# A graph kernel's second layer summed in transposed form in four PSUM banks, its first product moved ahead, its norm applied by ScalarE

## What is computed

```python
def layer_0(x, A, W1, b1, W2, b2):
    h = relu(A @ (x @ W1) + b1)
    return relu(A @ (h @ W2) + b2)

def layer_1(x, A, W1, W2, W3):
    A2 = A @ A; A3 = A2 @ A
    return (A @ x @ W1 + A2 @ x @ W2 + A3 @ x @ W3) / 3.0

x = layernorm(x + layer_0(x, adj, ...))     # over the 128 features, eps 1e-5
x = layernorm(x + layer_1(x, adj, ...))
```

## Time and profile before

| | value |
|---|---|
| median of three runs | 263.14 us |
| the profiled execution's own time | 263.5 us |
| its span, first to last instruction | 261.9 us |
| TensorE busy (1144 matmuls) | 245.7 us, 94% |
| VectorE busy | 204.5 us, 78% |
| ScalarE busy | 180.0 us, 69% |
| GpSimd busy | 11.8 us, 5% |
| moved by DMA | 19.43 MB, nearly all in the first 50 us |

### The profile page before, as it was taken

One profiled execution on the slowest core, in us unless ns is written; L12 is line 12 of the kernel. 1 busy time (PEld: TensorE's weight loads), 2 busy tenths in 40 slices (PEclk: granted clock), 3 DMA queues, 4 the chain that ended last, 5 costly groups with the idle time before them and its releaser, 6 DMA issues.

```text
span 261.9 us, 3653 instructions
## 1 busy us (share of the span) xinstructions
PE 245.7 (94%) x1144; PEld 201.4 (77%) x1144; DVE 204.5 (78%) x398; ACT 180.0 (69%) x302; POOL 11.8 (5%) x16
## 2 busy tenths in 40 slices
PE   0998999999999999999999999999999999999990
PEld 0766878787888867788888888888888888888870
DVE  1998888886777999999757595874796777779955
ACT  3889898987667658667766666776676677766520
POOL 1000000000000220220000000000000000022022
PEclk9999999999999999999999999999999999999998
DMA  5999999500000000000000000000000000001111
GB/s 165 372 404 406 403 404 406 219 3 0 0 0 4 1 0 0 0 3 0 1 0 4 0 0 0 3 0 0 1 3 1 0 3 0 0 0 41 43 40 40
DMA packets 10818, 19.43 MB, mean 74 GB/s; under 512 B 1200, under 2 KB 1712, under 8 KB 10800
## 3 DMA queue, kind: packets, MB, share of 16 engines
q1 hardware_dynamic: 10800, 19.21, 19.5%
HBM read 18.15 MB, written 1.05 MB: 73 GB/s over the span
## 4 chain that ended last, share of the span: by engine, by line
PE 79%; DVE 6%; SPq 4%; DMA 3%; issue 3%; POOL 2%; ACT 1%; POOLq 0%; DVEq 0%; ACTq 0%
PE sums L292 24%; PE sums L323 23%; PE sums L324 23%; PE weighted L280 5%; DMA adj<-a_t 3%; SPq L192 3%; DVE ring_low L509 2%; PE turned L277 2%; POOL rstd L225 2%; PE lifted L241 1%; DVE stats L434 1%; DVE nodes L450 1%; SPq L194 1%; SPq L200 1%; ACT ring_high L403 1%
## 5 line engine op out<-in xcount | busy, mean ns | idle before, releaser
L509 DVE TENSOR_TENSOR ring_low<-adj,ring_high 128x512 fp32r<-128x512 f32 x240 | 157.8, 687 | 43.1 <-PE sums L292 28.2
L403 ACT ACTIVATE ring_high<-adj 128x512 fp32r<-128x512 f32 x240 | 147.0, 630 | 36.5 <-PE sums L324 28.1
L323 PE MATMUL sums<-ring_high,operand_high 128*128 128x512 f32 x240 | 96.0, 400 | 7.1 <-DVE operand_low L464 6.9
L292 PE MATMUL sums<-ring_low,operand_high 128*128 128x512 f32 x240 | 94.5, 394 | 1.4 <-DVE ring_low L509 1.3
L324 PE MATMUL sums<-ring_high,operand_low 128*128 128x512 f32 x240 | 94.3, 393 | 0.0
L323 PEld LDWEIGHTS sums<-ring_high,operand_high 128*128 128x128 f32 x240 | 45.5, 190 | 17.1 <-DVE operand_low L464 7.9
L292 PEld LDWEIGHTS sums<-ring_low,operand_high 128*128 128x128 f32 x240 | 45.3, 189 | 12.7 <-DVE ring_low L509 3.0
L324 PEld LDWEIGHTS sums<-ring_high,operand_low 128*128 128x128 f32 x240 | 45.6, 190 | 9.0
L323 PE MATMUL sums<-resident_high,operand_high 128*128 128x512 f32 x80 | 33.2, 416 | 0.0
L292 PE MATMUL sums<-resident_low,operand_high 128*128 128x512 f32 x80 | 31.3, 391 | 0.0
L324 PE MATMUL sums<-resident_high,operand_low 128*128 128x512 f32 x80 | 31.2, 390 | 0.0
(11 more groups left out here) (34 smaller groups left out, 78.1 us busy)
## 6 DMA issues: line engine op xcount, KB each, us to landing
adj<-a_t SPq DMA_DIRECT2D x48, 256.0 KB, 9.1
resident_raw<-a_t SPq DMA_DIRECT2D x16, 256.0 KB, 9.2
nodes<-x_rows SPq DMA_DIRECT2D x4, 256.0 KB, 6.0
out_rows<-nodes SPq DMA_DIRECT2D x3, 256.0 KB, 2.5
out_rows<-nodes SPq DMA_DIRECT2D x2, 128.0 KB, 1.9
par<-params SPq DMA_DIRECT2D x1, 192.0 KB, 9.1
par<-params SPq DMA_DIRECT2D x1, 129.0 KB, 8.1
```

The costliest lines, as they stand in the source:

```text
L292: used = nc.tensor.matmul(sums[:, c, :], operand_high[:, hop % 2, k, :], a_low, start=False, stop=(k == TILES - 1))
L323: nc.tensor.matmul(sums[:, c, :], y_high, a_high, start=(k == 0), stop=False)
L403: nc.scalar.activation(ring_high[:, n % RING, :], adj[:, c, j * STREAMED + i, :], ACT.Copy).then_inc(high_ready, 1)
L509: nc.vector.tensor_tensor(ring_low[:, n % RING, :], adj[:, c, j * STREAMED + i, :], ring_high[:, n % RING, :].bitcast(F32), ALU.subtract). ...
```

## The change

Hop 0: x is loaded transposed together with W1 (`lead_in`), and TensorE forms x W1 first, 16 fp32 products of 128 x 128 in five groups of 1, 3, 4, 4 and 4 tiles (`X_GROUPS`). The group for tiles `first` to `last` is multiplied ahead of tile `first` - 2, and its high and low parts are made ahead of tile `first` - 1, straight from PSUM. The lifts and the separate relu are gone; the evacuation applies bias and relu, and the products by W2 come four tiles after the chunk. The first block of A is issued by ScalarE. `x_rows`, for the residual, is loaded after A. Nine fp32 products on a zeroed buffer (`WARM`) stand ahead of everything on TensorE.

Layer 1: the four banks `filters` collect W1ᵀ(A x)ᵀ + W2ᵀ(A² x)ᵀ in transposed form. For this hops 2 and 3 get one tile more per chunk (`WIDE`, a 17th, streamed): the chunk's sum is split from PSUM into a ring slot and multiplied by the split weight, three products of 128 x 512. The post of hop 2 is four transposes, that of hop 3 four products by W3, whose result is the operand of hop 4; hop 4 sums onto `filters`, its evacuation scales by 1/3, and its post is four transposes. The additions L429 of hops 2 and 3 are gone. Only hop 2 keeps the interleaved order of tiles.

All hops: a tile's three products are now issued together, operand low by A high, high by high, and then at once operand high by A low, with the wait for `low_ready` ahead of it.

Norm: VectorE also forms minus the mean; GpSimd forms a shift, minus the mean times rstd, after the power; ScalarE applies scale and shift to four node tiles (Identity with a scale and a bias read per partition) ahead of item 12. Only the last chunk's halves are still applied by VectorE.

```diff
+X_GROUPS = ((0, 1), (1, 4), (4, 8), (8, 12), (12, 16))
+WARM = 9
+def wide_after(hop, c):
+    return {(2, 0): 9, (2, 1): 11}.get((hop, c), 7)
 def post_step(hop, c):
-    return end_of(hop, c) + (SECOND_AFTER if hop == 0 else POST_AFTER[c])
+    return end_of(hop, c) + (8 if (hop, c) == (2, 1) else 4)
...
+            for n in range(whole_groups):
+                if n:
+                    pool.wait_ge(normalised, n)
+                root(n, slice(0, TPC))
+                pool.wait_ge(rstd_ready, n + 1)
+                nc.gpsimd.tensor_tensor(shift[:], neg_mean[:], rstd[:], ALU.mult).then_inc(shift_ready, 1)
...
+            def first_products(g):
+                pe.wait_ge(lead_sems[g], 16)
+                if g >= 2:
+                    pe.wait_ge(operand_low_ready, g - 1)
+                first, last = X_GROUPS[g]
+                for t in range(first, last):
+                    done = nc.tensor.matmul(x_bank(g)[:, t - first, :], lead[:, 1 + t, :], lead[:, 0, :],
+                                            start=True, stop=True)
+                done.then_inc(first_multiplied, 1)
...
+                nc.tensor.matmul(bank, y_low, a_high, start=first, stop=False)
+                used = nc.tensor.matmul(bank, y_high, a_high, start=False, stop=False)
+                if i < STREAMED:
+                    used.then_inc(high_used, 1)
+                    pe.wait_ge(low_ready, n + 1)
...
+                used = nc.tensor.matmul(bank, y_high, a_low, start=False, stop=last)
...
+            pe.wait_ge(warm_ready, 1)
+            for _ in range(WARM):
+                nc.tensor.matmul(turned[:, 0, :], chunk_t[:, 0:P], chunk_t[:, 0:P], start=True, stop=True)
...
+                        if max(first - 2, 0) == k or (first == 1 and k == 0):
+                            first_products(g)
...
+            def x_tiles(g):
+                first, last = X_GROUPS[g]
+                act.wait_ge(first_multiplied, g + 1)
+                nc.scalar.activation(operand_high[:, 0, first:last, :], x_bank(g)[:, 0:last - first, :], ACT.Copy
...
+            def norm_apply(hop, c):
+                act.wait_ge(shift_ready, residuals(hop, c))
+                for t in range(TPC):
+                    tile = nodes[:, c * TPC + t, :]
+                    last = nc.scalar.activation(tile, tile, ACT.Identity, bias=shift[:, t:t + 1],
+                                                scale=rstd[:, t:t + 1])
+                last.then_inc(normalised, 1)
...
+                for hop, c in posts(n, 5):
+                    if hop in NORMED:
+                        norm_apply(hop, c)
...
+                        if max(first - 1, 0) == k:
+                            x_tiles(g)
```

More of the change, by code:

```diff
@@ L30, with tile_order, all_steps @@
 ACT = mybir.ActivationFunctionType
[L32 to L41, removed]
-    early = TILES - TPC
[L43 to L52, removed]
+W2, B1, B2 = 0, D, D + 1
+V3 = B2 + 1
+PARAMS = V3 + D
+def tile_order(hop):
+    if hop != 2:
+        return [(hop, c, k) for c in range(CHUNKS) for k in range(TILES)]
+    early = TILES - TPC
+    order = [(hop, c, k) for c in (0, 1) for k in range(early)]
+    order += [(hop, c, k) for c in (0, 1) for k in range(early, TILES)]
+    return order + [(hop, c, k) for c in (2, 3) for k in range(TILES)]
+def wide_after(hop, c):
+    return {(2, 0): 9, (2, 1): 11}.get((hop, c), 7)
+def all_steps():
+    order = [step for hop in range(HOPS) for step in tile_order(hop)]
+    after = {order.index((hop, c, TILES - 1)) + wide_after(hop, c): (hop, c, WIDE)
+             for hop in (2, 3) for c in range(CHUNKS)}
+    steps = []
+    for at, step in enumerate(order):
+        steps.append(step)
+        if at in after:
+            steps.append(after[at])
+    return steps
+STEPS = all_steps()
 def streamed(k):
@@ L194, in load, with lead_part @@
                     sp.dma_start(resident_raw[:, c, j, :], a_t[c, :, k, :]).then_inc(resident_in[c][j], 16)
[L196 to L200, removed]
+            def lead_part(g):
+                first, last = X_GROUPS[g]
+                part = slice(first + (g > 0), last + 1)
+                sp.dma_start(lead[:, part, :], lead_in[:, part, :]).then_inc(lead_sems[g], 16)
+            lead_part(0)
+            for k in range(1, TILES):
+                if k == 1:
+                    lead_part(1)
+                elif k % TPC == 2 and k // TPC + 2 < len(X_GROUPS):
+                    lead_part(k // TPC + 2)
+                elif k == TILES - TPC:
+                    sp.dma_start(par[:, W2:V3], params[:, W2:V3]).then_inc(layer_0_in, 16)
                 load(0, k)
-            sp.dma_start(par[:, W1:V1], params[:, W1:V1]).then_inc(layer_0_in, 16)
             for c in range(1, CHUNKS):
@@ L222, in _, with root @@
             pool.wait_ge(exponent_ready, 1)
[L223 to L228, removed]
+            def root(n, part):
+                pool.wait_ge(variance_ready, n + 1)
@@ L232, in _ @@
+            for half in range(HALVES):
+                root(whole_groups + half, slice(half * half_tiles, (half + 1) * half_tiles))
         @block.tensor
         def _(pe):
-            def lift(c):
-                pe.wait_ge(chunk_evacuated, c + 1)
-                if c == 0:
-                    pe.wait_ge(layer_0_in, 16)
[L239 to L242, removed]
@@ L411, in _ @@
+                    nc.scalar.activation(ring_high[:, n % RING, :], source, ACT.Copy).then_inc(high_ready, 1)
+                    n += 1
+                elif hop == 0:
+                    act.wait_ge(resident_in[c][j], 16)
+                    nc.scalar.activation(resident_high[:, c, j, :], resident_raw[:, c, j, :], ACT.Copy
+                                         ).then_inc(resident_high_ready, 1)
+            for n in range(ITEMS, ITEMS + OVERHANG):
+                visits(n)
             act.wait_ge(chunk_summed, HOPS * CHUNKS)
```

434 lines of the change are left out of this document (212 added, 222 removed).

## The result

The changed kernel takes 265.96 us (median, 265.36 to 266.12) against 263.12 (263.04 to 263.2) of the kernel before: ratio 1.0104, 95% interval 1.0086 to 1.0121. It is slower by 1%; 264.7 was forecast. The profiled execution is the fastest of the four, 265.36 us with a span of 263.6. Its span is 1.7 us over that of before, where the sum of the prediction had 1.6.

The account below looks back on a forecast made before the run. TensorE, busy 94% of the span, was taken to bound the kernel. The four parts, 0.1 - 2.15 + 3.75 - 0.1 = +1.6 us on the median of 263.14, gave 264.7 us, range 259.6 to 267.2.

Parts of the forecast that it names:

- Part 1: Start and hop 0: removed lifts and warm-up pay for x W1 and its loop between engines; +0.1 us.
- Rival (b): Chunk 0: the x loop costs nothing as loads hold TensorE there anyway; 2.8 us less, 261.9 us; chance 0.12.
- Part 2: Counted TensorE work after hop 0: fourth lift gone, wide tiles added, posts cheaper; -2.15 us.
- Part 3: Norms of hops 1 and 4: application on ScalarE delays ring items, TensorE waits; 5.6 against 1.85 before, +3.75 us.
- Rival (a): Norm: chain short enough, stalls only 1.0 to 2 us in all; 260.6 us; chance 0.28.
- Rival (d): Norm: Identity needs another activation table, two loads per norm, 14 in all; about 280 us; chance 0.02.
- two things eat this: Hop 1 norm's 0.4 us spare: eaten by item 14's low product standing 0.69 us earlier and by application on ScalarE.
- the power's earlier start: Norm on GpSimd: VectorE, freed of 1.12 us, starts the residual earlier; power starts at 4.6 instead of 5.0 us.
- the one wait of 1.25 us for item 14: Each hop 1 norm: TensorE waits 1.25 us for item 14's low part, some 10.4 us after the post.
- Part 4: Tail: transposes replace products ahead of the residual, minus the mean added ahead of two variances; -0.1 us.
- (c): Hop 0: VectorE falls behind or the clock drops before the first sum; 2.5 us later, 267.2 us; chance 0.08.
- (e): Products sharing operand high: second weight load saved, 328 x 0.014 = -4.5 us, 260.2 us; chance 0.04.

Follow-up runs that it names:

- x_earlier: The changed kernel with the products x W1 of the last three groups issued one tile earlier (ahead of tile first-3): 263.85 us, 1.0019 of before.
- before_warm: The kernel before with nine warm-up products on zeroed data ahead of the first sum: 263.26 us, 0.9997 of before.
- no_wide: The changed kernel without the eight wide tiles, leaving out the W1 and W2 terms in layer 1: 260.18 us.
- apply_vector: The changed kernel with the norm applied by VectorE again, without minus the mean and the shift: 260.36 us, 0.9891 of before.
- low_behind: The changed kernel with each tile's low product again behind the next tile's two others: 264.04 us, 1.0026 of before.
- vector_x_behind: The changed kernel with norm on VectorE, x W1 one tile earlier and low product behind the next tile's others: 256.32 us, 0.9729 of before.

## Why the prediction was right, by its steps

**Part 1.** First sum at 7.04 (7.3 to 8.1 in six other profiles), 7.6 forecast. Chunk 0 ends at 24.47 (first post 27.19 less four tiles), 24.4 forecast; hop 0 at 59.83, 59.8 forecast. The gap at tiles 3, 7 and 11 is there, and `x_earlier` shows its cause: 2.1 us less with the products one tile earlier. Rival (b), a loop that costs nothing, fell by this. That the end of chunk 0 fits to 0.1 us is in part luck. A group of four tiles takes 4.8 us (12.12, 16.91 and 21.71 us in the trace) where 4.6 was summed, so from the first sum to its end chunk 0 takes 17.4 us and not 16.8, and this execution happened to start its sums 0.6 us early. The excess is in the stands for the resident tiles, 0.67 us for the high part and 0.24 for the low one, each with 0.11 more on the product behind: 1.1 us a group, not 0.95. The list of what was removed counts slow products with 1.6 us; `before_warm` shows that they cost nothing in the kernel before. The sum does not use that 1.6, as it builds chunk 0 anew.

**Part 2.** From the first post of hop 2 to the last product: 255.40 - 133.24 = 122.16 us after, less hop 4's 0.7 of waits, 121.5; before 253.49 - 130.81 = 122.7, less 0.2 of waits in hop 4, 122.4. That is -1.0 us; the sum without the fourth lift had -1.3. `no_wide` prices the wide tiles at 5.8 instead of 5.45, which is the missing 0.3. The starts around a wide tile are 0.229 to 0.235 us apart, so small gaps where one kind of product follows another make up at least part of it.

**Part 3.** The power starts 4.69 us after the post (forecast 4.6), the shift takes 0.31 us and is 0.35 from its start to the application's (0.35 forecast), the application runs from 6.44 to 8.09 (6.35 to 8.0), and 5.7 us are lost in hops 1 and 4 against `apply_vector` (5.6). So the term is right in place and size. Rival (a) fell. Rival (d) fell too: the profile has one table load, of 1.28 us at the start. By the Trainium skill, "ScalarE: Activation LUTs", section "Table sets: the hidden batching unit", Identity is in every set, and the trace agrees. The Identity's 483 ns agree with the Trainium skill, "ScalarE: Activation LUTs", section "What ACT_TABLE_LOAD costs": an estimate from its 186 ns, 0.833 ns for each of 128 elements and 93 ns for each of two per-partition operands is 479 ns.

What failed within part 3 is a sentence about its parts: "two things eat this". The nearer place of the low product is not half of it. `low_behind` gave 0.3 us of 5.0 in hop 1, because the high parts behind the application are late as well. With the application on VectorE the order is worth little there too: behind hop 0 `vector_x_behind` is 0.3 us shorter than `apply_vector`. Only the first of two serial limits had been walked to the end; the walk with the low parts freed was not made.

The reason given for the power's earlier start failed as well, though its number came out. The forecast had 4.6 instead of 5.0 us because VectorE would be freed of the application. In `apply_vector` VectorE has the application again, and the power starts at 4.5. What the two kernels share is the plain order of tiles in hop 1, with norms a whole chunk apart; before, the residual of chunk 3 started 1.77 us after its post, after that 1.23. No run tests that order alone. And the one wait of 1.25 us for item 14 is three shorter waits that add up to about as much.

**Part 4.** From the last product to the end of the span 8.17 us after (255.40 to 263.57), 8.45 before (253.49 to 261.93): -0.3, forecast -0.1 with bounds of -0.3 to +0.2. Profiles whose tail has the same operations differ by 0.2 us in it.

**Rivals (c) and (e).** Nothing falls behind in hop 0 beyond chunk 0: 11.79 us from post to post. Nor did the clock drop in the gap ahead of the first sum: TensorE is idle for 1.19 us there, and the products behind it start 0.23 to 0.34 us apart, where 1.2 GHz shows as 0.43. Products that share operand high stand 0.23 us apart as before, and there are as many weight loads as products (1146): no load is saved.

**The point forecast** was 1.26 us too low. 0.6 of it is the distance from the profiled execution to the median, which the start may explain but no trace shows. The forecast had carried over the 0.36 us of the kernel before, whose profiled execution lay above its median, and that has the other sign. The remaining 0.3 is the sum itself: +1.6 forecast and +1.9 measured between the two profiled executions.

## What to carry to other kernels

Work moved to the engine with the lower busy share still costs if it stands ahead of a ring's next items in that engine's queue: walk the queue from the event that it waits for to the last item whose deadline it touches, against the ring's depth. Walk it again with the first late part made free, since the next late part may be just behind it; and a small edit that feeds one engine from another (x W1) needs its distance in the order counted in tiles, both ways. Three prices, of 5.6 us (the application), 2.1 us (the distance of x W1) and some 2 us (the order of products), hid in a change whose counted work was a gain.

## What was not expected of the hardware

In the kernel before with Identity on ScalarE, TensorE was idle 1.9 us ahead of 101.01; from 101.80 the products stand 0.43 us apart until 104.79 (1.2 GHz, a granted clock of 0.50 in 101.80 to 104.80), then 0.23 again. So the loss there was the wait and about 1.9 us of slow products behind it (eight distances of 0.43 and two of some 0.37, against 0.23). The length of the idle time alone does not tell when this happens. In hop 4 of the same execution TensorE stood as long for the same evacuation, and the products behind went on 0.23 us apart, at 2.4 GHz (a granted clock of 1.00 in 252 to 256):

```profile
251.96 1.16 PE L283 MATMUL weighted<-par,chunk_t 128*128 128x128 f32 x8 [1.84 <-ACT chunk_t L358]
252.88 0.48 PE L326 MATMUL sums<-ring_high,operand_high 128*128 128x512 f32 x1
253.19 0.39 PE L327 MATMUL sums<-ring_high,operand_low 128*128 128x512 f32 x1
253.42 0.40 PE L295 MATMUL sums<-resident_low,operand_high 128*128 128x512 f32 x1
```

The idle 0.8 us ahead of the first lift, in this kernel and in the one before, had no slow stretch behind it either. One difference stands in the trace: ahead of the long wait in hop 1 TensorE had already been idle for 0.82 us, at 95.82, and at the same place in hop 4 for only 0.08 us. Whether that decided it is not shown.

The nine warm products, too, end differently from one execution to the next. They begin at 1.05 us each time. In the profile of the changed kernel the last two of their eighteen records and all records of x W1 behind them are already 0.11 us apart; in `low_behind` the four products x W1 behind them still have 0.21 between their records. With that the first sum moves from 7.04 to 8.12 us.
